# Two layer norms of the next stage moved from the tail of a stage into its attention loop

## The reference

```python
x = x + attn(layernorm(x))      # qkv projection, causal softmax attention, output projection
x = x + ffn(layernorm(x))       # 1024 -> 64, an own 1-16-1 relu net for each of the 64, 64 -> 1024
def _layernorm(x, axis=-1, eps=1e-5):
    m = jnp.mean(x, axis=axis, keepdims=True)
    v = jnp.var(x, axis=axis, keepdims=True)
    return (x - m) / jnp.sqrt(v + eps)
```

## Time and profile before

| | us |
|---|---|
| profiled execution, device time | 4308.04 |
| its span, slowest core (core 7) | 4306.1 |
| spans of the 8 cores | 4295.1 to 4306.1 |
| runs without profile | 4349.8 and 4473.83 |
| their median | 4411.82 |

### The profile page before, as it was taken

How to read it: one execution, slowest core, us unless ns; L and a number is a source line. 1 busy time by engine, 2 the same in 40 slices (tenths; PEclk the granted TensorE clock), 3 DMA queues, 4 the chain that set the end, 5 groups by cost and what they waited for, 6 DMA issues and landing times.

```text
span 4306.1 us, 41301 instructions; the slowest of 8 cores (4295.1 to 4306.1 us)
## 1 busy us (share of the span) xinstructions
PE 2762.4 (64%) x12288; PEld 1067.5 (25%) x12288; DVE 1110.5 (26%) x2486; ACT 1850.3 (43%) x3201; POOL 167.6 (4%) x324
## 2 busy tenths in 40 slices
PE   0657576586656658577674756757666575765874
PEld 0222232232222223232231312223222132322321
DVE  3141311401323141230323223031132413214112
ACT  0424337166141625518523261743733234272581
POOL 0000000000000000000000000000000000000000
PEclk9868687697676868778776776878877676786886
DMA  6010000100101010010000001000000000000000
GB/s 199 15 36 20 25 25 18 42 6 16 39 20 39 15 35 15 16 39 11 20 30 30 30 20 40 11 25 25 15 25 28 32 25 25 30 15 30 10 11 25
DMA packets 39249, 122.09 MB, mean 28 GB/s; under 512 B 9786, under 2 KB 9914, under 8 KB 39036
## 3 DMA queue, kind: packets, MB, share of 16 engines
q0 software_dynamic: 21504, 67.13, 4.3%
q1 hardware_dynamic: 17020, 51.80, 4.0%
q10 hardware_dynamic: 512, 0.53, 0.0%
HBM read 85.34 MB, written 34.08 MB: 28 GB/s over the span
## 4 chain that ended last, share of the span: by engine, by line
PE 49%; ACT 17%; issue 12%; DVE 11%; DMA 10%; ACTq 1%; DVEq 0%; SPq 0%; POOLq 0%
PE P L315 10%; PE P L390 9%; ACT s_probs L362 7%; PE P L442 7%; DMA s_zz<-zscr 6%; PE P L292 6%; PE P L353 5%; ACT s_zz L413 3%; ACT s_zz L410 3%; DVE s_xln L220 2%; DMA zscr<-s_zz 2%; DVE s_probs L485 2%; DVE s_x L453 2%; PE P L537 2%; PE P L541 2%
## 5 line engine op out<-in xcount | busy, mean ns | idle before, releaser
L362 ACT ACTIVATE s_probs<-P 128x1024 bf16<-128x1024 f32 (+3 forms) x1280 | 1063.0, 895 | 283.2 <-PE P L357 231.7
L353 PE MATMUL P<-s_q,s_k 64*128 64x512 bf16 (+3 forms) x1280 | 464.9, 392 | 519.5 <-ACT s_probs L362 485.6
L390 PE MATMUL P<-s_probs,s_vaug 128*65 128x512 bf16 (+3 forms) x2560 | 710.6, 399 | 93.2 <-DVE s_probs L370 49.8
L370 DVE TENSOR_TENSOR s_probs<-s_probs,s_tril 128x256 bf16<-128x256 bf16 x512 | 145.8, 292 | 1400.9 <-ACT s_probs L362 1398.0
L442 PE MATMUL P<-s_ow,s_comb 128*128 128x512 bf16 x1024 | 335.3, 486 | 236.8 <-DVE s_comb L422 197.6
L357 PE MATMUL P<-s_q,s_k 64*128 64x512 bf16 (+3 forms) x1280 | 474.1, 399 | 0.0
L315 PE MATMUL P<-s_xlnT,s_wqk 128*128 128x512 bf16 x2048 | 444.8, 379 | 0.0
L390 PEld LDWEIGHTS P<-s_probs,s_vaug 128*65 128x65 bf16 x2560 | 244.9, 120 | 449.9 <-issue 354.9
L238 ACT ACTIVATE s_stats<-s_stats 128x1 f32<-128x1 f32 x128 | 37.7, 294 | 738.2 <-DVE s_stats L235 738.2
L474 PE MATMUL P<-s_id,s_xln 128*128 128x128 bf16 x512 | 106.9, 257 | 371.8 <-ACT s_probs L481 276.3
L422 DVE TENSOR_TENSOR s_comb<-P,s_zz 64x512 bf16<-64x512 f32 x256 | 174.9, 683 | 631.6 <-DMA s_zz<-zscr 631.4
(11 more groups left out here) (58 smaller groups left out, 1966.8 us busy)
## 6 DMA issues: line engine op xcount, KB each, us to landing
s_x<-x SPq DMA_DIRECT2D x64, 512.0 KB, 3.6
s_zz<-zscr POOLq DMA_DIRECT2D x256, 128.0 KB, 2.8
out<-s_x POOLq DMA_DIRECT2D x64, 512.0 KB, 2.9
s_x<-wqk_t SPq DMA_DIRECT2D x16, 512.0 KB, 7.1
s_x<-wv_t SPq DMA_DIRECT2D x8, 512.0 KB, 6.2
s_x<-ow_t SPq DMA_DIRECT2D x8, 512.0 KB, 6.3
zscr<-s_zz ACTq DMA_DIRECT2D x256, 2.0 KB
s_x<-bias_rows SPq DMA_DIRECT2D x1, 260.0 KB
```

Source lines behind the costliest of these rows:

```text
L353: s.op("pe", lambda E, c=hp, k=kt, c0=col0, S=SC: E.matmul(S[:, c0:512], s_k[0:64, c * T + k * 128: c * T + (k + 1) * 128], s_q[0:64, c * ...
L362: texp = s.op("act", lambda E, S=SC, pb=prb, c0=col0: E.activation(pb[:, :].rearrange("p (h c) -> p h c", h=2, c=512)[:, :, c0:512], S.rea ...
L390: P=pv_banks[bank]: E.matmul(P[:, c0:512], s_vaug[:, ti * NH * 65 + hh2 * 65: ti * NH * 65 + hh2 * 65 + 65], pb[:, hi2 * 512 + c0: hi2 * 5 ...
```

## The change

`attention` gets a `hook`, called with u at the end of each unit, after the unit's divisions have been put into the lists. The hook puts `LN(0)` there at the end of unit 0 and `LN(1)` at the end of unit 1. The two calls in the tail go. `LN(2)`, `LN(3)` and all `TR` stay. In the last stage there is no next stage, and `LN` does nothing. In `emit_ln`, L235 gets one dependency more: the ScalarE exponential of the last layer norm that used the same columns of `s_stats`.

```diff
@@ attention
-        def attention(sq, g):
+        def attention(sq, g, hook=None):
...
                         st_["pv_done"][bank] = tcm
                         comb_written.append(tcm)
+                if hook is not None:
+                    hook(u)
@@ emit_ln
-                s_stats[:, cMS:cMS + 1], ALU.mult, ALU.subtract), deps=[tsq, tms])
+                s_stats[:, cMS:cMS + 1], ALU.mult, ALU.subtract),
+                deps=[tsq, tms, st_["lnA_act"].get(scol)])
...
                 scale=-0.5), deps=[tsr])
+            st_["lnA_act"][scol] = trc
@@ the loop over stages
-            comb = attention(sq, g)
...
+            def hook(u):
+                if u < 2:
+                    LN(u)
+
+            comb = attention(sq, g, hook)
...
-            LN(0)
             epilogueA(sq, g, 0, slot(0), comb)
             TR(0, 0)
             epilogueA(sq, g, 1, slot(1), comb)
             TR(0, 1)
             epilogueB(sq, g, 0, slot(0))
-            LN(1)
             epilogueA(sq, g, 2, slot(2), comb)
```

More of the change, by code:

```diff
@@ L215, in build_program @@
             "txl": {},
+            "lnA_act": {},
         }
```

## The result

| | kernel before | changed kernel |
|---|---|---|
| median of all runs, us | 4309.2 (10 runs) | 4500.8 (11 runs) |
| fastest run, us | 4305.8 | 4496.5 |
| ratio after/before, 95% interval | | 1.0431 [1.0401, 1.0461] |
| profiled execution, us | 4308.0 | 4498.9 |
| mean span of the 8 cores in it, us | 4302.0 | 4492.1 |

The change makes the kernel 4.3% slower, by 190 us. The two runs of the kernel before that stood ahead of the prediction, 4349.8 and 4473.8, were not typical: seven of the other eight lie between 4305.8 and 4311.3. Some executions have one die at a lower clock; all comparisons here are between executions without that, or between the cores of the other die.

What follows compares the result with a forecast made beforehand. No engine is full; what counts is who waits for whom, mainly TensorE for ScalarE's exponentials. Delays of 170.3 + 48.9 us, tail and clock 0, make 219 us; on the faster run shown, 4349.8, that gives 4570, range 4495 to 4710.

Steps and rivals of the forecast that it cites:

- T: In the attention: the end of the fourth division of a unit, the zero point for the forecast's times in us.
- T + 3.96: End of units 0 and 1: the next unit's first exponentials (L362) would start then, in place of T - 5.19.
- T + 9.16 and T + 8.92: Exponential of key tile 2 behind a hook: g of 1 or more 7.74 us later, g = 0 6.11 us later.
- The sum of the delays: Key tile 2 at all hooks: 22 x 7.74 = 170.3 us plus 8 x 6.11 = 48.9 us, together 219 us.
- L353's idle time for L362: Sign in the profile after: TensorE's wait for ScalarE's exponentials should grow by some 200 us.
- The clock term: TensorE's clock after the longer pause, relative to key tile 2: no change taken; bounds -19 and +52 us.
- the upper bound: TensorE's clock up to two periods later (+1.74 us) at each of 30 hooks: +52 us.
- The low bound of the cost: Whole kernel: 219 - 19 (clock) - 10 (tail) = 190 us.
- Rival 1: Tail: VectorE would be the bound, so removing 30 x 5.01 = 150 us there gives 4200; chance 0.02.
- Rival 2: Unit boundaries: the four exponentials have slack behind T, so nothing changes, 4350 to 4412; chance 0.03.
- rival 3: Unit boundaries: only the layer norm's own time is paid, 30 x 3.93 = 118 us, 4468; chance 0.05.
- Rival 4: TensorE after the hooks: the longer pause costs clock too, 4350 + 271 = 4621; chance 0.2.

Runs made afterwards that it cites:

- the version that costs nothing: Against the kernel before: both layer norms in the attention, statistics ahead of the first division, scaling ahead of the third; ratio 0.9982 [0.9948, 1.0015].
- waits kept: Changed kernel with L413's wait on an earlier division issued in units 1 to 3 although already passed; ratio to the kernel before 1.0480 [1.0461, 1.0499].

## Why the prediction was right or wrong

**Which step failed.** The direction and the mechanism were right, and what failed is the size of the sum and the time it was put on. Two terms of the sum were mis-sized: the clock, put at 0, gave back 14 to 18 us, and the stretch from the last exponential to T, not in the sum at all, gave back 8.9 us. And the cost was added to 4349.8, the wrong time. The three are taken one by one below.

**The direction and the mechanism were right.** The hold of ScalarE's queue was replayed as T + 3.96 for the first exponentials and came out at T + 3.89 (median of the hooks). Key tile 2 was forecast at T + 9.16 and T + 8.92 and measured at T + 9.10 and T + 8.78. The sum of the delays was put at 219 us, and 217.3 were measured at that point.

**The removal from the tail is worth 0**, as taken. The tails of both kernels add up to 1493.3 us, and the experiment without the two layer norms confirms it. Loads and the new dependency of L235 left no trace. The sign "L353's idle time for L362 should grow by some 200 us" was 266 us. It counts TensorE's pause, which starts before T: 30 x (16.4 - 7.5) = 267.

One wording was too narrow. The prediction explains the hold by ScalarE's two operations standing "ahead of the first exponentials of the next unit". They stand at the same place in the version that costs nothing; the hold needs VectorE's statistics to stand behind the fourth division as well, which the prediction's replay (T + 0.03 + 3.83) does count.

**The clock term was mis-sized.** The text listed "the clock could be back one period earlier (-0.87)" and took 0, with the reason that TensorE works without a gap from T + 6 on as it does now from T on. That reason looked at the wrong stretch. In the earlier trace rows the restart begins at 428.29, before T, and has a gap of 1.22 us ahead of 432.45; in the changed kernel there is none. The step from key tile 2 to 3 shrank by 13.6 us in sum over the 22 boundaries. Another 4 us came back elsewhere, about 2 of them in units without a hook, and no run shows that these are the clock's. So the term is between -14 and -18, and the bound of -19 was the better value. The sentence drawn from "TensorE: Matmul & The Clock Gate" of the Trainium skill, section "Part 1: The HAM clock gate", was read as pointing to the upper bound, because the pause is longer. The measurement points the other way: after both pauses, 7.54 and 16.4 us, TensorE restarts at the lower level, and what differs is the work after the restart. That the clock rises with sustained work agrees with the runs (0.68 over 453 to 459 us in the changed kernel, 0.50 over 455 to 462 with a gap put in); it was the application that was wrong.

**A term was missing:** -8.9 us between the last exponential and T. The text held that everything behind key tile 2 is shifted as it is. Some 7 us of this is the wait that the hook makes superfluous in ScalarE's queue, as the experiment that keeps it showed.

**The base was wrong.** The predicted 4570 was the cost put on 4349.8, "the faster of the two". Added to the profiled execution's 4308.0 it would have been 4527. The other runs show that 4308 was the typical time. The median of 4500.8 lies just inside the range 4495 to 4710, and the ratio applied to the kernel before, 4309.23 x 1.0431 = 4494.96, just below it. Of the 69 us between 4570 and 4501, some 41 come from the base (4349.8 against 4309.2) and 27 from the two terms above.

**Luck.** The low bound of the cost, 190 us, is what was measured, but not for its reasons: it took 10 us off for the tail, which gave nothing, and did not have the 9 us of the denominators.

**The rivals.** Rival 1, with the rule of the Trainium skill ("Perfetto Trace Analysis", section "Optimization Strategy") that interleaving regimes may help, fell at the tail: there was nothing to gain. For LN(3), moved from a stretch that VectorE bounds into waits of VectorE, mixing the two did pay, 76 us of the tails a core. Rival 2 (hidden) and rival 3 (only the layer norm's own time, 118 us) fell with the result, and the experiment that waits for T alone shows why: without VectorE's statistics in the hold it still costs 95 us. Rival 4 (the clock comes back later) fell; it comes back sooner.

## What to carry to other kernels

Where an engine takes its instructions in order, the cost of moving an operation is what stands behind it in the queue while it waits for its input, and not its duration: two operations of ScalarE of 0.5 us together held it for 8.7 us. So look at the other engine's queue, the one that makes the input. Here ScalarE's order was the same in the costly and in the free version; it was enough to put VectorE's statistics ahead of the divisions, into a wait of VectorE, in place of behind them. And before work is moved away from a place, take it out altogether once and see whether that place gets shorter at all.

## What was not expected of the hardware

TensorE's clock after a pause depends here on whether the restart has a gap. After a pause of 7.5 us and a restart with a gap of 1.0 us (medians), key tiles 2 and 3 are 2.81 us apart (the lower level, 1.2 GHz). After 13.2 or 16.4 us and a gapless restart the medians are 1.95 and 1.89. After 16.4 us with a gap of 1.16 us put in it is 2.81 again.

A wait on a semaphore that had long been reached still costs: four of them on ScalarE, one for each denominator, lengthen the four pairs from 6.59 to 6.75 us, 0.04 us each (changed kernel and "waits kept").
